# Weights loaded first, the mask cast in one VectorE copy per chunk, and GpSimd normalising all graphs from the third group on

## What is computed

```python
def _direction(x, W, Wg, b, bg, adj, rel_ids):
    h = x @ W.T
    g = h @ Wg.T
    vals = (h[:, :, None, :] + b) * jax.nn.sigmoid(g[:, :, None, :] + bg)
    onehot = (adj[..., None] == rel_ids).astype(h.dtype)
    return jnp.einsum('bnmr,bmrd->bnd', onehot, vals)
...
out = _direction(node, W_fwd, Wg_fwd, b_fwd, bg_fwd, adj_mat, rels)          # relations 2 to 40
out = out + _direction(node, W_bwd, Wg_bwd, b_bwd, bg_bwd, adj_t, rels)
out = out + _direction(node, W_loop, Wg_loop, b_loop, bg_loop, adj_t, rel1)  # relation 1
...
h = jnp.maximum(_layernorm(x, axis=-1), 0.0)
x = x + jax.nn.relu(out)      # of node = h
```

## Time and profile before

| | us |
|---|---|
| median of three runs | 113.37 |
| lowest and highest run | 111.84, 114.14 |
| profiled execution, its own time | 112.11 |
| its span | 110.3 |
| busy in the span: TensorE | 98.8 (90%) |
| VectorE | 94.0 (85%) |
| ScalarE | 91.8 (83%) |
| GpSimd | 87.1 (79%) |

### The profile page before, as it was taken

The page is one execution under the profiler, slowest core; times in us unless marked ns, Lnnn a source line. Parts: engine busy times, 40 slices in busy tenths (PEclk is TensorE's granted clock), DMA queues, the critical chain, the costliest instruction groups (busy, mean ns, idle before and its releaser), DMA issues.

```text
span 110.3 us, 2526 instructions
## 1 busy us (share of the span) xinstructions
PE 98.8 (90%) x780; PEld 92.1 (83%) x780; DVE 94.0 (85%) x202; ACT 91.8 (83%) x153; POOL 87.1 (79%) x182
## 2 busy tenths in 40 slices
PE   5524789899999999999999999999999999999970
PEld 1113569789999999999999999999999999999960
DVE  1508529899999999999999999999999999897780
ACT  4137533999999999999999999999999999999650
POOL 2380790999999999999999999999999999995000
PEclk9999999999999999999999999999999999999999
DMA  2999999999999999999999999980606050515067
GB/s 73 281 311 281 286 290 291 292 291 292 291 317 311 343 332 321 320 320 321 305 320 301 260 309 274 317 222 6 190 6 190 6 180 10 158 38 176 14 185 207
DMA packets 50275, 25.48 MB, mean 231 GB/s; under 512 B 850, under 2 KB 50260, under 8 KB 50260
## 3 DMA queue, kind: packets, MB, share of 16 engines
q1 hardware_dynamic: 49968, 25.17, 81.6%
q10 hardware_dynamic: 292, 0.13, 0.5%
HBM read 16.91 MB, written 8.39 MB: 229 GB/s over the span
## 4 chain that ended last, share of the span: by engine, by line
PE 80%; DMA 5%; POOL 3%; DVE 3%; issue 2%; ACT 2%; ACTq 1%; DVEq 0%; POOLq 0%
PE psum L750 23%; PE psum L715 16%; PE psum L728 14%; PE psum L729 13%; PE psum L733 13%; DMA w_raw<-in_L_gnn_Wg_loop 5%; POOL rstd L309 1%; DVE x_all L560 1%; DVE stats L500 1%; POOL xn L324 1%; PE psum L691 1%; ACT xn L393 1%; ACT hT_hi L404 1%; ACT L374 1%; PE psum L688 0%
## 5 line engine op out<-in xcount | busy, mean ns | idle before, releaser
L728 PE MATMUL psum<-w_hi,hT_hi 128*128 128x256 f32 x128 | 35.1, 307 | 1.8 <-issue 0.8
L750 PE MATMUL psum<-vals,mask 128*128 128x128 f32 x256 | 33.6, 275 | 0.0
L411 ACT ACTIVATE psum<-bias_all 128x1024 f32<-128x1024 f32 x32 | 32.9, 1027 | 0.1
L324 POOL TENSOR_SCALAR xn<-x_all,mean_neg,rstd 128x128 f32<-128x128 f32 x75 | 32.8, 449 | 0.1
L729 PE MATMUL psum<-w_lo,hT_hi 128*128 128x256 f32 x128 | 32.4, 285 | 0.0
L750 PEld LDWEIGHTS psum<-vals,mask 128*128 128x128 f32 x256 | 31.2, 191 | 0.1
L728 PEld LDWEIGHTS psum<-w_hi,hT_hi 128*128 128x128 f32 x128 | 24.7, 193 | 2.8 <-issue 1.7
L309 POOL TENSOR_TENSOR rstd<-var_eps,minus_half 128x8 f32<-128x8 f32 (+1 forms) x17 | 26.6, 1564 | 0.0
L500 DVE BATCH_NORM_STATS2 stats<-x_all 128x6 f32<-128x256 f32 x64 | 23.9, 416 | 2.7 <-DMA x_all<-in_x 2.7
L535 DVE TENSOR_TENSOR vals<-psum,gate 128x512 f32<-128x512 f32 (+1 forms) x33 | 21.7, 659 | 4.3 <-ACT gate L426 4.2
L729 PEld LDWEIGHTS psum<-w_lo,hT_hi 128*128 128x128 f32 x128 | 24.8, 193 | 0.0
(11 more groups left out here) (34 smaller groups left out, 34.2 us busy)
## 6 DMA issues: line engine op xcount, KB each, us to landing
adj_all<-in_adj SPq DMA_DIRECT2D x16, 512.0 KB, 6.6
x_all<-in_x SPq DMA_DIRECT2D x15, 512.0 KB, 6.7
out<-x_all SPq DMA_DIRECT2D x15, 512.0 KB, 4.4
x_all<-in_x SPq DMA_DIRECT2D x2, 256.0 KB, 3.1
out<-x_all SPq DMA_DIRECT2D x1, 256.0 KB, 2.5
out<-x_all SPq DMA_DIRECT2D x2, 128.0 KB, 2.5
w_raw<-in_L_gnn_W_loop ACTq DMA_DIRECT2D x1, 64.0 KB, 3.2
w_raw<-in_L_gnn_Wg_loop ACTq DMA_DIRECT2D x1, 64.0 KB, 5.3
```

The source lines that it names most:

```text
L324: last = pool.tensor_scalar(xn[:, s, j * D:j * D + D], x_all[:, g * GC + j * D:g * GC + j * D + D], mean_neg[:, p, k:k + 1], rstd[:, p, k: ...
L411: nc.scalar.activation(prod_ps[s].rearrange("p g a d -> p g (a d)"), bias_all[:, :, :].rearrange("p a d -> p (a d)").unsqueeze(1) .to_broa ...
L728: nc.tensor.matmul(to, hi, w_hi[:, :], start=False, stop=False, skip_group_check=True)
L750: last = nc.tensor.matmul(to[:, j * D:j * D + D], mask[:, g % MASKS, j * N:j * N + N], vals[:, s, j * D:j * D + D], start=True, stop=True)
```

## The change

Three things are changed. First, ScalarE's queue carries the weights alone, and the two bias rows go through SyncE's queue behind the first x tile; ScalarE's weight copies come ahead of the first `seed`; filler matmuls on zeros (`keep_busy`) are put between the first TensorE steps. Second, GpSimd no longer casts the mask: VectorE casts a whole chunk's mask (1024 elements per partition) in one instruction. Third, ScalarE normalises no graph, VectorE three graphs each of groups 0 and 1, and GpSimd one of each of these and all four from group 2 on. The negated mean and the shift fall away: the normalise subtracts the mean that lies in `stats`, which now has four slots. At the end the store of the first half of the last group goes through ScalarE's queue.

```diff
@@ -196,17 +192,14 @@
         def live(g):
             return 0 <= g < GROUPS
 
-        def shares(g):
-
-            if g < 2:
-                return range(0), range(0, 2), range(2, 4)
-            if g % 2 == 0:
-                return range(0, 3), range(3, 4), range(4, 4)
-            return range(0, 2), range(2, 3), range(3, 4)
-
-        def act_norms(g):
-
-            return g + 1 if g < 2 else 2 + (g - 1) // 2
+        def pool_share(g):
+
+            return 1 if g < 2 else GROUP
+
+        def mean_of(g, j):
+
+            k = g % CHUNK * GROUP + j
+            return stats[:, g // CHUNK % STAT_SLOTS, k // 2, 1 + k % 2 * 3:2 + k % 2 * 3]
 
         def parts(g):
 
...
@@ -236,6 +229,8 @@
                 load_tile(adj_all, adj, c * CG, c * CC, CG, adj_loaded[c])
 
             load_tile(x_all, x, 0, 0, GROUP, x_first)
+            sp.dma_start(bias_row[0:1, 0, :], b_loop).then_inc(bias_loaded, 16)
+            sp.dma_start(bias_row[0:1, 1, :], bg_loop).then_inc(bias_loaded, 16)
             load_tile(x_all, x, GROUP, GC, CG - GROUP, x_loaded[0])
             load_x(1)
...
-            sp.wait_ge(half_out, 1)
-            store_tile((GROUPS - 1) * GROUP, (GROUPS - 1) * GC, GROUP // 2)
             sp.wait_ge(out_ready, GROUPS)
             store_tile(B - GROUP // 2, (B - GROUP // 2) * D, GROUP // 2)
 
...
-            def coefficients(p, lo, hi, var_done, pow_done, at, done):
-
-                st = stats[:, p, lo // 2:hi // 2, :].rearrange("p k (e f) -> p k e f", e=2)
+            def coefficients(c, lo, hi, var_done, at, done):
+
+                p = c % 2
+                st = stats[:, c % STAT_SLOTS, lo // 2:hi // 2, :].rearrange("p k (e f) -> p k e f", e=2)
                 pool.tensor_scalar(var_eps[:, p, lo:hi].rearrange("p (k e) -> p k e", e=2), st[:, :, :, 2],
...
-                pool.tensor_scalar(mean_neg[:, p, lo:hi].rearrange("p (k e) -> p k e", e=2), st[:, :, :, 1],
-                                   -1.0, 0.0, ALU.mult, ALU.add)
                 pool.wait_ge(var_done, at)
                 pool.tensor_tensor(rstd[:, p, lo:hi], var_eps[:, p, lo:hi], minus_half[:, lo:hi], ALU.pow
-                                   ).then_inc(pow_done, 1)
-                pool.wait_ge(pow_done, at)
-                pool.tensor_tensor(shift[:, p, lo:hi], mean_neg[:, p, lo:hi], rstd[:, p, lo:hi], ALU.mult
                                    ).then_inc(done, 1)
...
-                if g % CHUNK == 0:
+                if g == 0:
+                    pool.wait_ge(first_coef, 1)
+                elif g % CHUNK == 0 or g == 1:
...
-                for j in shares(g)[0]:
+                for j in range(pool_share(g)):
...
-                        mean_neg[:, p, k:k + 1], rstd[:, p, k:k + 1], ALU.add, ALU.mult)
+                        mean_of(g, j), rstd[:, p, k:k + 1], ALU.subtract, ALU.mult)
                 last.then_inc(normed_pool, 1)
-
-            def edges(g):
-
-                if g % CHUNK == 0:
-                    pool.wait_ge(adj_loaded[g // CHUNK], 16)
-                if g >= MASKS:
-                    pool.wait_ge(summed, g - (MASKS - 1))
-                pool.tensor_copy(mask[:, g % MASKS, :], adj_all[:, g * GC:g * GC + GC]
-                                 ).then_inc(mask_ready, 1)
 
...
-                    pool.wait_ge(normed_dve, (c - 1) * CHUNK)
-                    pool.wait_ge(normed_act, act_norms((c - 1) * CHUNK - 1))
-                coefficients(c % 2, GROUP if c == 0 else 0, CG, var_ready, pow_ready, c + 1, coef_ready)
+                    pool.wait_ge(normed_dve, CHUNK)
+                coefficients(c, GROUP if c == 0 else 0, CG, var_ready, c + 1, coef_ready)
...
             pool.wait_ge(first_stats, 1)
-            coefficients(0, 0, GROUP, first_var, first_pow, 1, first_coef)
+            coefficients(0, 0, GROUP, first_var, 1, first_coef)
+            normalise(0)
             chunk_coefficients(0)
+            normalise(1)
             chunk_coefficients(1)
             normalise(2)
-            edges(0)
             normalise(3)
             for t in range(GROUPS):
                 if t % CHUNK == 0 and live(t + 4):
                     chunk_coefficients((t + 4) // CHUNK)
-                if live(t + 1):
-                    edges(t + 1)
                 if live(t + 4):
                     normalise(t + 4)
...
-            act.dma_start(bias_row[0:1, 0, :], b_loop).then_inc(bias_loaded, 16)
-            act.dma_start(bias_row[0:1, 1, :], bg_loop).then_inc(bias_loaded, 16)
             act.dma_start(w_raw[:, 0, :], W_loop).then_inc(w_loaded, 16)
             act.dma_start(w_raw[:, 1, :], Wg_loop).then_inc(w_loaded, 16)
-
-            def normalise(g):
...
+            act.wait_ge(w_turned, 1)
+            nc.scalar.activation(w_gT[:, :], bank[6][:, 128:256], ACT.Copy).then_inc(w_gT_ready, 1)
+            nc.scalar.activation(w_hi[:, 0:D], bank[6][:, 0:D], ACT.Copy).then_inc(w_hi_ready, 1)
             act.wait_ge(bits_set, 1)
             act.wait_ge(bias_ready, 1)
             seed(0)
-            act.wait_ge(w_turned, 1)
-            nc.scalar.activation(w_gT[:, :], bank[6][:, 128:256], ACT.Copy).then_inc(w_gT_ready, 1)
-            nc.scalar.activation(w_hi[:, 0:D], bank[6][:, 0:D], ACT.Copy).then_inc(w_hi_ready, 1)
             act.wait_ge(w_turned, 2)
             nc.scalar.activation(w_hi[:, D:2 * D], bank[7][:, 0:D], ACT.Copy).then_inc(w_hi_ready, 1)
-            normalise(0)
...
             seed(1)
             act.wait_ge(half_ready, 1)
             relu_turned(0)
-            normalise(1)
             sigmoid(0)
             relu_turned(1)
             for t in range(GROUPS):
-                if live(t + 3):
-                    normalise(t + 3)
...
+            act.wait_ge(half_out, 1)
+            act.dma_start(
+                out[B - GROUP:B - GROUP // 2, :, :].rearrange("b n d -> n b d"),
+                x_all[:, (B - GROUP) * D:(B - GROUP // 2) * D].rearrange("p (b d) -> p b d", b=GROUP // 2)
+            ).then_inc(stored, 16)
...
-                if g % CHUNK == 0 and c >= 2:
-                    dve.wait_ge(coef_ready, c - 1)
+                if g % CHUNK == 0 and c >= STAT_SLOTS:
+                    dve.wait_ge(normed_pool, (c - STAT_SLOTS + 1) * CHUNK)
...
-                for j in shares(g)[1]:
...
-                        mean_neg[:, c % 2, k:k + 1], rstd[:, c % 2, k:k + 1], ALU.add, ALU.mult)
+                        mean_of(g, j), rstd[:, c % 2, k:k + 1], ALU.subtract, ALU.mult)
                 last.then_inc(normed_dve, 1)
+
+            def edges(c):
+
+                dve.wait_ge(adj_loaded[c], 16)
+                if c * CHUNK >= MASKS:
+                    dve.wait_ge(summed, c * CHUNK - MASKS + CHUNK)
+                s = c * CHUNK % MASKS
+                nc.vector.tensor_copy(mask[:, s:s + CHUNK, :].rearrange("p g n -> p (g n)"),
+                                      adj_all[:, c * CC:c * CC + CC]).then_inc(mask_ready, 1)
 
...
             row_stats(0)
             row_stats(1)
+            normalise(0)
             split_weights(0)
-            normalise(0)
             split_weights(1)
             row_stats(2)
             row_stats(3)
@@ -579,18 +547,17 @@
             normalise(1)
             messages(0)
             low_part(1)
-            normalise(2)
             row_stats(4)
+            edges(0)
             row_stats(5)
-            normalise(3)
             low_part(2)
             row_stats(6)
             for t in range(1, GROUPS + 1):
                 if live(t):
                     messages(t)
-                if live(t + 3):
-                    normalise(t + 3)
                 output(t - 1)
+                if (t + 1) % CHUNK == 0 and live(t + 1):
+                    edges((t + 1) // CHUNK)
                 if live(t + 2):
                     low_part(t + 2)
                 if live(t + 6):
...
+
+            def keep_busy(times, where):
+
+                for _ in range(times):
+                    nc.tensor.matmul(bank[where][:, 0:256], zeros[:, 0:128], zeros[:, 0:256], start=True, stop=True)
+
+            keep_busy(3, 1)
             pe.wait_ge(ones_ready, 1)
...
             turn_weights(w_raw[:, 0, :], w_raw[:, 1, :], w_gT[:, :], w_turned, w_gT_ready, 1)
+            keep_busy(3, 1)
...
-                if shares(g)[0]:
-                    pe.wait_ge(normed_pool, g - 1)
-                pe.wait_ge(normed_dve, g + 1)
-                if shares(g)[2]:
-                    pe.wait_ge(normed_act, act_norms(g))
+                pe.wait_ge(normed_pool, g + 1)
+                pe.wait_ge(normed_dve, min(g + 1, CHUNK))
...
-                pe.wait_ge(mask_ready, g + 1)
+                pe.wait_ge(mask_ready, g // CHUNK + 1)
...
             turn_rows(0)
+            keep_busy(5, 1)
             pe.wait_ge(w_lo_ready, 2)
             products(0)
             turn_rows(1)
+            keep_busy(4, 6)
             products(1)
             turn_rows(2)
```

More of the change, by code:

```diff
@@ L32, in build @@
     XN = 4
+    STAT_SLOTS = 4
     ctx = ExitStack()
```

(29 more changed lines are left out.)

4 lines of the change are left out of this document (1 added, 3 removed).

## The result

| | before | after |
|---|---|---|
| median of the runs, us | 113.75 (4 runs) | 148.91 (4 runs) |
| lowest and highest, us | 111.84, 114.39 | 148.31, 149.99 |
| span of the profiled execution, us | 110.3 | 147.2 |
| chunk (two groups), us | 5.71 | 8.54 |

The ratio is 1.32, with a 95% interval of 1.304 to 1.344: slower by a third. Some runs of the kernel before are in a slower state, so every ratio here compares fast runs alone. The forecast was 111.7 with a range of 108.3 to 114.8, so it was wrong, and in its main term.

A forecast was written before the change was run, and what follows sets the result against it. VectorE, GpSimd and TensorE were taken to bound the kernel together, within 0.1 us of each other per chunk. Start -3.0, chunks +1.8 and end -0.4 gave -1.6: 110.5, scaled to 111.7 us, range 108.3 to 114.8.

The forecast's parts named there:

- its main term: Steady part: a chunk of two groups goes from 5.71 to 5.85 us, +1.8 us over 13 chunks.
- three normalises come, 1.25: GpSimd per chunk: casts, negated mean and shift go (1.50), three normalises come (1.25), leaving 5.47 of 5.72 us.
- my upper bounds: Steady part: VectorE's cast at most 1.13 us, its wait for GpSimd 0.42, GpSimd's wait for the cast 0.60.
- my slower rival: VectorE's cast streams at the plain rate and still waits for GpSimd: chunk 6.26, scaled time 117.2, chance 0.09.
- VectorE's cast: VectorE per chunk: one mask cast of 1024 elements comes in, costing 0.60 us, plus 0.20 waiting for GpSimd.
- the plain rate: VectorE's cast at 1.04 ns an element, from its statistics rows: 1.13 us for 1024 elements, the upper bound.
- waits for a GpSimd instruction in flight: VectorE's normalise form, SBUF to SBUF with one tensor input, waits for running GpSimd instructions: 0.60 instead of 0.33 us.
- The clash on GpSimd: Steady part: GpSimd's next normalise waits for VectorE's cast, 0.40 us a chunk, bringing GpSimd to 5.87.
- The start: Before the steady part: earlier weights, earlier fast pace and changed shares save 3.0 us, bounds -1.5 and -4.
- The end: Last three stores: the middle one on ScalarE's queue saves issue time on SyncE, taken as -0.4 us.
- My figure for TensorE: Steady part: TensorE needs 2.81 us from one L715 to the next, 5.62 per chunk.

The follow-up runs named there:

- the kernel with add: The changed kernel with add in place of subtract in GpSimd's normalise alone (values then x plus mean): 110.85 us, ratio 0.993 to the kernel before.
- the negation on ScalarE: The changed kernel with add, VectorE's mask cast moved ahead of the messages, and the mean negated by ScalarE once per chunk: 106.84 us, ratio 0.955.

## Why the prediction was wrong, and where it was right

**The step that failed** is the price of GpSimd's normalises: "three normalises come, 1.25", GpSimd 5.47 a chunk. I priced the new form by the row of the old one. The order before and after shows the same name, TENSOR_SCALAR, with the same shapes, and neither a row nor the order says which operations are in it; the diff does, and I read ALU.subtract as a change of sign. Measured, eight of them take 6.2 to 6.7 instead of 3.4, and a chunk 8.54 instead of 5.85. On the 5.71 of before that is 13 x 2.83 = 36.8 us; the spans differ by 36.9. Neither my upper bounds nor my slower rival (6.26 a chunk, from a slow cast) touched it: the row of before did not show this form. I gave the cast, which no row showed either, two bounds; this term got none.

**VectorE's cast**: forecast 0.60; 0.62 from start to start in the kernel with add. Right, and the plain rate (1.13) is out. That it waits for GpSimd, 0.20, is wrong: in the steady part it was held by 0.02 with add and 0.04 with subtract. The reading behind it, that such an instruction "waits for a GpSimd instruction in flight", is too wide, and the earlier trace rows show it: the normalise at 53.13 takes its usual 0.33 with two GpSimd normalises in flight (52.50 to 53.38). In the whole trace before, the 14 VectorE normalises that start under a GpSimd cast take 0.49 to 0.60, and the 14 that start under a GpSimd normalise 0.33 to 0.34. In these traces it is the cast, on either engine, that holds the other one's instruction.

**The clash on GpSimd**: forecast 0.40 a chunk, by a mechanism no row of before showed in this direction; 0.45 in the kernel with add, and 0.50 taken back by moving the cast. Right in kind and nearly in size. The chunk without the subtract is 5.90, my forecast 5.85. In the kernel as changed it falls in every second chunk only.

**The start**: forecast -3.0, with bounds of -1.5 and -4; it was -3.7 (23.5 to 19.8). The weights' transpose was forecast at 6.7 and stood at 5.46, ReLU(0) at 10.3 and stood at 8.89. The rows of the changed kernel:

```profile
1.23 0.53 ACTq L356 DMA_DIRECT2D w_raw<-in_L_gnn_Wg_loop  x1
...
5.46 0.47 PE L655 MATMUL psum<-ident,w_raw 128*128 128x128 f32 x1
...
7.74 1.06 PE L687 MATMUL psum<-ident,xn 128*128 128x128 f32 x4
...
8.89 0.60 ACT L364 ACTIVATE hT_hi<-psum 128x512 fp32r<-128x512 f32 x1 [0.24 <-PE psum L687]
```

The gating weight is issued 0.74 earlier, as worked out, but is used 1.99 earlier. I had carried the issue's gain over to the arrival one to one; that it also lands sooner, 2.9 us after its issue instead of 5.3, was left out. TensorE no longer waits for it: the transpose stands right behind the bias matmul, which waits 0.62 for the second bias row on SyncE's queue and starts at 4.34. The bias rows gate TensorE's first steps now. At the fast pace I erred the other way: 1.5 credited, 0.9 to 1.0 measured by leaving the fillers out. In the kernel as changed the start's gain cannot be seen at group 4 (23.34), because fourteen slow normalises lie before it on GpSimd.

**The end**: forecast -0.4, measured -0.03. I credited the time of issuing; what ended last was the last store itself and what follows it, and that was not shortened.

**The sum without the one word**: forecast a span of 110.3 - 1.6 = 108.7; the kernel with add has 109.1. All other terms together missed by 0.4 us, but partly by luck: the steady part cost 0.6 more than forecast, the start gave 0.7 more and the end 0.4 less.

**My figure for TensorE**, 5.62 a chunk, which I gave as its need, is not a floor: it is 5.55 with the negation on ScalarE. The weight loads show the room, 9.62 of 10 us before and 19.96 of 20 there. A floor read from steps between rows of an engine that waits now and then is too high.

## What to carry to other kernels

An instruction's price belongs to its operation too, not only to engine, shape and operands: when a diff changes the operation on an engine, no row of the old one prices it, and a chance must be kept for it in proportion to how often it runs. On GpSimd, negate the small operand once and add, rather than subtract per element; and place a VectorE cast from SBUF to SBUF so that one long GpSimd instruction on few elements starts before it and ends after it. When an engine was at the bound with no gap, ask what a doubling of each of its new instructions would do before asking about waits.

## What the hardware showed that I had not expected

- GpSimd's two-operation form on float32 with a subtract takes 3.5 ns an element, with add 0.92 ns; 0.778 against 0.428 us for 128. Subtract in the second place costs the same, 0.80 long. VectorE's takes 0.34 with either.
- A VectorE cast of 1024 elements holds a GpSimd normalise for 0.45 to 0.52 us and is itself hardly ever held. A power of 8 elements runs under it at its usual 1.64 if it ends after the cast; if not, it ends 0.04 after it (12 of 12). An 8-element operation that started under a cast took 0.64 instead of 0.20.
- Fifteen matmuls on zeros in the first 12.4 us, eleven of them ahead of the first products, brought the fast pace into these products, for a gain of 0.9 to 1.0 us.

In the slow kernel the granted clock from 40 to 50 us is 0.83 where it was 1.00. That is a mean over two levels, in the same columns:

```profile
36.00:40.80 4.80, 2.60 (x25) 2.41 (x23) 3.28 (x7) 1.95 (x3) 4.70 (x6) 1.00 1.11 331
40.90:44.20 3.30, 3.30 (x18) 3.30 (x17) 1.36 (x3) 2.00 (x3) 3.22 (x6) 0.50 1.11 323
```

From 40.9 to 44.2 us it is at the lower level (0.50, 1.2 GHz), after 4.8 us in which TensorE was busy 2.60; from 44.3 to 50 it is at the upper one again. The chain runs through GpSimd (85%), so this follows from the slow normalises and does not make the loss. With add, and with the negation on ScalarE, it is 1.00.
